# A one-core decoder layer: expert weights loaded during attention, and the two down projections of a step on separate halves of the array

## The reference, cut to what matters

```python
logits = x @ gate_w.T                      # 64 experts
topv, topi = jax.lax.top_k(logits, 8)
rw = softmax(topv)                         # weights of the 8 chosen
gu = einsum('nh,eih->nei', x, gu_w)        # gate and up, 64 + 64 columns per expert
inter = silu(gate) * up                    # 64 values per token and expert
out = einsum('nei,ehi->nh', inter_w, dp_w) # down projection, 64 -> 256
out = out + sigmoid(x @ sh_gate1_w.T) * (shared expert, same shapes)
```

## Time and profile before

| | us |
|---|---|
| median of 3 runs | 1806.1 (1800.71 to 1807.99) |
| the profiled execution, whole | 1804.36 |
| its span, first to last instruction | 1802.4 |
| PE busy | 1475.3 (82%) |
| VectorE busy | 1319.6 (73%) |
| GpSimd busy | 1109.3 (62%) |
| ScalarE busy | 694.7 (39%) |

### The profile page before, as it was taken

The page is one execution under the profiler, slowest core; times in us unless marked ns, Lnnn a source line. Parts: engine busy times, 40 slices in busy tenths (PEclk is TensorE's granted clock), DMA queues, the critical chain, the costliest instruction groups (busy, mean ns, idle before and its releaser), DMA issues. The chain is left out here.

```text
span 1802.4 us, 34145 instructions
## 1 busy us (share of the span) xinstructions
PE 1475.3 (82%) x9600; PEld 1233.7 (68%) x9600; DVE 1319.6 (73%) x3879; ACT 694.7 (39%) x1462; POOL 1109.3 (62%) x1090
## 2 busy tenths in 40 slices
PE   3679999999999899999999855779999999992000
PEld 2568888888888787888888744567777777771000
DVE  3458888888888888888888843147777765553898
ACT  3235444545453444444443412124444444441221
POOL 3328676767676667677776641027777777774444
PEclk8789999999999999999999977579999999996555
DMA  5861212121212112121212117976655556642886
GB/s 197 287 201 50 84 49 77 54 79 51 76 56 74 56 63 69 53 79 47 85 47 71 45 70 230 256 214 191 188 187 185 184 182 189 190 120 99 294 298 241
DMA packets 161421, 237.36 MB, mean 132 GB/s; under 512 B 28044, under 2 KB 135578, under 8 KB 156836
## 3 DMA queue, kind: packets, MB, share of 16 engines
q1 hardware_dynamic: 127636, 160.73, 29.2%
q0 software_dynamic: 27648, 69.28, 10.4%
q10 hardware_dynamic: 6032, 6.13, 1.0%
HBM read 127.47 MB, written 116.93 MB: 136 GB/s over the span
## 5 line engine op out<-in xcount | busy, mean ns | idle before, releaser
L1347 POOL DMA_INDIRECT expert_out_scratch<-y,target x320 | 319.1, 997 | 225.5 <-issue 107.4
L484 POOL DMA_INDIRECT slot_scratch<-xrow x256 | 272.2, 1063 | 187.8 <-DVE xrow L1100 111.6
L1438 ACT ACTIVATE x_turned<-bank_x 128x512 f32<-128x512 f32 x176 | 105.1, 597 | 281.1 <-PE bank_x L1377 281.0
L523 PE MATMUL bank_c<-wq_w,x1t 128*128 128x512 f32 x768 | 193.2, 403 | 15.4 <-DVE q_work L942 11.7
L1417 PE MATMUL bank_y<-dp,inter_t 64*128 (+1 forms) x704 | 205.7, 414 | 0.0
L1396 PE MATMUL bank_g<-gu,x_turned 128*128 (+1 forms) x1408 | 195.6, 284 | 0.0
L669 PE MATMUL bank_d<-wo_w,o2t 128*128 128x256 f32 x1536 | 193.4, 286 | 2.0 <-DVE o2t L858 2.0
L669 PEld LDWEIGHTS bank_d<-wo_w,o2t 128*128 128x128 f32 x1536 | 187.6, 192 | 3.1 <-DVE o2t L858 2.7
L1616 DVE COPY y<-bank_y 128x512 f32<-128x512 f32 x160 | 110.6, 691 | 97.1 <-PE bank_y L1417 97.1
L429 POOL TENSOR_TENSOR q_rs<-q_ve,minus_half 128x8 f32<-128x8 f32 x64 | 137.4, 2147 | 71.3 <-DVE q_ve L933 67.6
L523 PEld LDWEIGHTS bank_c<-wq_w,x1t 128*128 128x128 f32 x768 | 142.3, 190 | 56.6 <-DVE q_work L942 21.0
(11 more groups left out here) (232 smaller groups left out, 3074.0 us busy)
## 6 DMA issues: line engine op xcount, KB each, us to landing
x_rows<-slot_scratch SPq DMA_DIRECT2D x320, 136.0 KB
rows<-expert_out_scratch SPq DMA_DIRECT2D x32, 1152.0 KB, 5.6
slot_scratch<-zeros SPq DMA_DIRECT2D x18, 1088.0 KB, 11.8
gu<-in_gate_up SPq DMA_DIRECT2D x11, 768.0 KB, 12.5
expert_out_scratch<-y,target POOLq DMA_INDIRECT x320
token_row_scratch<-xrow SPq DMA_DIRECT2D x32, 136.0 KB, 1.8
x_rows<-token_row_scratch SPq DMA_DIRECT2D x16, 272.0 KB
dp<-in_down SPq DMA_DIRECT2D x22, 192.0 KB, 13.7
```

Source lines behind the costliest of these rows:

```text
L484: nc.gpsimd.indirect_dma_start(out=slot_d[:, :], out_offset=bass.IndirectOffsetOnAxis(ap=xrow[slot][:, SLOT8 + k:SLOT8 + k + 1].bitcast(U3 ...
L523: last = nc.tensor.matmul(target, left[a][:, c, :], right(b, c), start=(n == 0 and c == 0), stop=(n == len(PASSES) - 1 and c == C - 1))
L1347: nc.gpsimd.indirect_dma_start(out=y_d[:, :], out_offset=bass.IndirectOffsetOnAxis(ap=target[s % 8][:, j:j + 1], axis=0), in_=y[s % 4][:, ...
L1438: nc.scalar.activation(xt[s % 2][:, :, :, :].rearrange("p j c n -> p (j c n)"), bank_x[:, s % 2, :], ACT.Copy).then_inc(sig["x_copied"], 1)
```

## The change

Six edits go together.

1. **Place of the weights.** `gu` and `dp` are given fixed places in SBUF that overlap attention's big buffers (the query, key and value weights, `wo_w`, `o2t`, `q_work`); attention's buffers are declared in another order for it.
2. **Time of the loads.** SP loads all of `gu` at the iteration of attention in which tile 31 is projected, after the last projections, and all of `dp` at the iteration in which tile 31 is stored, after the last output projection; in both cases ahead of that iteration's `store_row` and `store_meta`. No weights are loaded by the expert phase's opening; its first steps wait on `gu_in` and `dp_in`.
3. **Two halves.** `dp` now has 128 partitions. Partitions 0 to 63 hold all 66 down matrices; partitions 64 to 127 hold a ring of 8, one per step modulo 8, and the shared expert's. The second row tile of each sparse step takes its down matrix from the ring. SP loads it with the step's rows: a third DMA per sparse step (64 rows of 1 KB, from a row index that is a second column of the table). The gated values of both row tiles are turned by one transpose of 128 x 128 instead of two of 128 x 64, so the two lie on the two halves of the partitions.
4. **`bank_y`.** Each row tile's result has a bank of its own, so there is one buffer, and `project(s)` waits for the copy of step s-1.
5. **Waits.** A row buffer's reload waits for `y_ready` of its step as well (the ring). POOL no longer waits for the row scatters at the end of attention; SP waits for them before the first sparse load.
6. **Order in the expert phase.** The tables are computed in DVE's iterations 0 to 2 instead of 0 to 6, with a third find per column for the ring's rows and four small operations more. The loads of `metas` and `slots` are issued after step 1 instead of before step 0.

```diff
+            def load_gate_up():
+                sp.wait_ge(sig["qk_projected"], TILES)
...
+                sp.wait_ge(sig["v2_projected"], TILES)
+                groups = gu[:, 0:EPAIRS * 512].rearrange("p (g n) -> p g n", g=GROUPS)
+                for g in range(GROUPS):
+                    sp.dma_start(groups[:, g, :], gate_up[g, :, :]).then_inc(weights["gu_in"], 16)
+
+            def load_down():
+                sp.wait_ge(sig["q_transposed"], 2 * TILES)
+                sp.wait_ge(sig["cross_proj"], TILES)
+                own = dp[0:INNER, :].rearrange("p (g a h n) -> p g a h n", g=GROUPS, a=GROUP, h=2)
+                for g in range(GROUPS):
+                    for h in range(2):
+                        sp.dma_start(own[:, g, :, h, :],
+                                     down[g, h * INNER:(h + 1) * INNER, :].rearrange("p (a n) -> p a n", a=GROUP))\
+                          .then_inc(weights["dp_in"], 16)
+                sp.dma_start(dp[INNER:P, 8 * D:9 * D], down[GROUPS - 1, 0:INNER, 2 * D:3 * D])\
+                  .then_inc(weights["dp_in"], 16)
...
                 at(b, store_x1)
+                if c is not None and isinstance(c.n, int) and c.n == TILES - 1:
+                    load_gate_up()
+                if e is not None and isinstance(e.n, int) and e.n == TILES - 1:
+                    load_down()
                 at_slot(e, store_row)
                 at(e, store_meta)
...
             pipeline(pool, step, ahead=ahead)
-            for slot in range(2):
-                pool.wait_ge(sig[f"scattered{slot}"], 16 * TOP_K * (TILES // 2))
...
-        dp = sb("dp", [INNER, 2, EPAIRS, D])
+        sb("dp_home", [P, DP_W])
...
-        inter_t = [sb(f"inter_t{n}", [INNER, 2 * P]) for n in range(2)]
+        inter_t = [sb(f"inter_t{n}", [P, P]) for n in range(2)]
...
                 if s >= 8:
                     sp.wait_ge(sig["x_turned"], s - 7)
+                    if sparse(s):
+                        sp.wait_ge(sig["y_ready"], s - 7)
...
             def load_sparse(s):
...
+                at = sp.snap(regs[3], min_val=0, max_val=(GROUPS * P - INNER) * GROUP + GROUP - 1)
+                sp.dma_start(dp[INNER:P, s % 8 * D:(s % 8 + 1) * D], down_rows[bass.ds(at, INNER, GROUP), :])\
+                  .then_inc(done, 16)
...
-                for j in range(2):
-                    mm = nc.tensor.transpose(bank_i[0:INNER, s % 2, j * P:(j + 1) * P], inter[s % 2][:, j, :],
-                                             identity[:, :])
-                mm.then_inc(sig["inner_turned"], 1)
+                nc.tensor.transpose(bank_i[:, s % 2, 0:P], inter[s % 2][:, :, :].rearrange("p j x -> p (j x)"),
+                                    identity[:, :]).then_inc(sig["inner_turned"], 1)
...
             def project(s):
...
                 pe.wait_ge(sig["inner_copied"], s + 1)
-                if s >= 2:
-                    pe.wait_ge(sig["y_copied"], s - 1)
-                for j in range(2):
-                    first = held[s][j][1] if sparse(s) else shared_at[1]
-                    mm = nc.tensor.matmul(bank_y[:, s % 2, j * D:(j + 1) * D], inter_t[s % 2][:, j * P:(j + 1) * P],
-                                          dp_flat[:, bass.ds(first, D)], start=True, stop=True)
-                mm.then_inc(sig["y_ready"], 1)
+                if s >= 1:
+                    pe.wait_ge(sig["y_copied"], s)
+                own = held[s][1] if sparse(s) else shared_at[1]
+                ring = s % 8 if sparse(s) else 8
+                nc.tensor.matmul(bank_y[:, 0, 0:D], inter_t[s % 2][0:INNER, :], dp[0:INNER, bass.ds(own, D)],
+                                 start=True, stop=True)
+                nc.tensor.matmul(bank_y[:, 1, 0:D], inter_t[s % 2][INNER:P, :], dp[INNER:P, ring * D:(ring + 1) * D],
+                                 start=True, stop=True).then_inc(sig["y_ready"], 1)
...
-            tables = {0: [table_counts, table_whole, table_tiles], 3: [table_opened, lambda: table_find(0)],
-                      4: [lambda: table_find(1), lambda: table_find(2)], 5: [table_depth, table_rows], 6: [table_starts]}
-            for n in range(2):
-                tables[1 + n] = [lambda k=k: table_scan(k) for k in range(3 * n, 3 * n + 3)]
+            tables = {0: [table_counts, table_whole, table_tiles] + [lambda k=k: table_scan(k) for k in range(6)],
+                      1: [table_opened] + [lambda c=c: table_find(c) for c in range(3)],
+                      2: [table_depth, table_rows, table_starts]}
```

More of the change, by code:

```diff
@@ L27 @@
 GROUPS = EPAIRS // GROUP
-GROUP = 3
-GROUPS = EPAIRS // GROUP
 XW = 272
@@ L210, in attention_phase @@
         h2_rs = sb("h2_rs", [P, 1])
-        xrow = [sb(f"xrow{n}", [P, XW]) for n in range(2)]
         zeros = sb("zeros", [P, XW])
@@ L1230, in expert_phase, with number @@
         bank_x, bank_g, bank_i, bank_y = bank("bank_x", 2), bank("bank_g", 2), bank("bank_i", 2), bank("bank_y", 2)
+        later = SHARED_STEPS - SHARED_FIRST
+        order = [("shared", k) for k in range(SHARED_FIRST)]
+        for n in range(SPARSE_STEPS):
+            order.append(("sparse", n))
+            if later and n % 16 == 15 and n // 16 < later:
+                order.append(("shared", SHARED_FIRST + n // 16))
+        steps_of = {step: s for s, step in enumerate(order)}
         def sparse(s):
-            return s >= SHARED_STEPS
+            return order[s][0] == "sparse"
+        def number(s):
+            return order[s][1]
         def y_free(s):
+            uses = sum(order[k][0] == order[s][0] for k in range(s % 4, s + 1, 4))
             if sparse(s):
-                return sig[f"y_scattered{s % 4}"], 32 * ((s - SHARED_STEPS) // 4 + 1)
-            return sig[f"y_stored{s % 4}"], 16 * (s // 4 + 1)
+                return sig[f"y_scattered{s % 4}"], 32 * uses
+            return sig[f"y_stored{s % 4}"], 16 * uses
         def rows_loaded(s):
-            return sig[f"x_in{s % 8}"], 32 * (s // 8) if sparse(s) else 16 * (s // 8 + 1)
+            return sig[f"x_in{s % 8}"], sum(48 if sparse(k) else 16 for k in range(s % 8, s + 1, 8))
         block = stack.enter_context(nc.Block())
@@ L1306, in _ @@
[L1306 to L1314 removed]
+                    at = sp.snap(regs[2 * j], min_val=1, max_val=SLOT_ROWS - P)
@@ L1315, in _ @@
                     pass_tables()
                     sp.wait_ge(sig["tables_in"], 48)
-                if s >= SHARED_STEPS - 8:
-                    load_sparse(s + 8)
-            for s in range(SHARED_STEPS + 8, STEPS):
+                    for slot in range(2):
+                        sp.wait_ge(scattered[slot], 16 * TOP_K * (TILES // 2))
                 load_sparse(s)
+            for s in range(8):
+                load(s)
+            for s in range(STEPS):
+                if not sparse(s):
+                    store_shared(s)
+                if s + 8 < STEPS:
+                    load(s + 8)
+                if s == 1:
+                    sp.dma_start(metas[:, :, :], meta_d.rearrange("(t p) e -> p t e", p=P))\
+                      .then_inc(sig["metas_in"], 16)
+                    sp.dma_start(slots[:, :, :], row_d[:, SLOT8:SLOT8 + TOP_K].bitcast(U32)
+                                 .rearrange("(t p) k -> p t k", p=P)).then_inc(sig["slots_in"], 16)
@@ L1321, in _ @@
             for n in range(4):
-                sp.wait_ge(sig[f"y_stored{n}"], 16 * (SHARED_STEPS // 4))
+                sp.wait_ge(sig[f"y_stored{n}"], 16 * sum(not sparse(s) for s in range(n, STEPS, 4)))
         @block.gpsimd
@@ L1392, in gate_and_up @@
                 for j in range(2):
-                    first = held[s][j][0] if sparse(s) else shared_at[0]
+                    first = held[s][2 * j] if sparse(s) else shared_at[0]
                     for c in range(C):
@@ L1652, in _ @@
                     stage()
-                if s == SHARED_STEPS:
+                now = s < STEPS and sparse(s)
+                if now and number(s) == 0:
                     table_slots()
-                if sparse(s) and s < STEPS:
+                if now:
                     match_row(s)
@@ L1662, in _ @@
                     copy_y(s - 3)
-                if sparse(s) and s < STEPS:
+                if now:
                     bound_row(s)
-                n = s - SHARED_STEPS - 8
+                n = number(s) - 8 if now else None
                 if n == -1:
```

210 lines of the change are left out of this document (113 added, 97 removed).

## The result

| | before | after |
|---|---|---|
| median, us | 1807.05 (4 runs) | 1751.49 (4 runs, 1746.26 to 1757.51) |
| ratio to before | | 0.9687, 95% interval 0.9654 to 0.9719 |
| profiled execution, us | 1804.36 | 1752.66 |
| opening of the expert phase | 1094.5 | 1102.3 |
| opening to first scatter | 105.9 | 67.9 |

The account below looks back on a forecast made before the run. PE was taken to bound the sparse stage, with POOL close behind, and full DMA engines the shared stage. 1804.4 less 37 (shared) and 21 (sparse) gives 1746, 1748 us on the median's scale; range 1730 to 1772.

Parts of the forecast that it names:

- PE's step: Sparse step on PE: 2.75 us less 0.44 for down products and 0.11 for one transpose, giving 2.20.
- The step from the cross-attention rows to two products per step: Down products: halves run side by side as in cross-attention's four products, so four records take 0.62 us, 0.44 less.
- Rival 4: Down products: the halves don't overlap, PE needs 2.64 us a step, result 1754; chance 0.05.
- Sparse stage: POOL sets the pace: 160 x 2.56 plus 96 x 0.10 us makes 419, 21 less than 440.
- the collisions: Sparse stage: DVE lookups falling on POOL's scatter openings cost 0.10 us in each of 96 steps, bounds 0 and 0.19.
- Rival 1: Sparse stage: POOL keeps 2.75 us a step or worse in the 96 lookup steps, result 1757 to 1782; chance 0.12.
- The ring on SP: Third DMA per sparse step: SP needs 2.3 us a step, at most 2.73; row loads land in under 10, hidden.
- Rival 2: Sparse stage: SP becomes the bound through the third DMA, 2.73 us a step, result 1766; chance 0.08.
- Shared stage: Weights leave it, tables decide: first scatter at 1163 instead of 1200.5, 37 us saved; bounds 1154 and 1180.
- Rival 3: Shared stage hardly shrinks: table chain and SP's order set it, first scatter 1185, result 1770 us; chance 0.06.
- The end of attention: Early loads hidden there; tail costs 0, bounds 0 and a 2.6 us gain from POOL's dropped wait.
- Rival 5: Sparse stage: TensorE's clock falls as PE idles; half the steps slow adds 144 us, result 1892; chance 0.04.

Follow-up runs that it names:

- run 3: Changed kernel with one scatter per sparse step, the second row block's y never scattered: 1699.0 us (total not comparable), sparse stage 371.7 us.
- run 9: Changed kernel with the loads of metas and slots issued by POOL instead of SP: 1748.0 us, ratio 0.9636 to the kernel before.
- run 1: Changed kernel with the early weight loads kept and the halves undone: 1780.2 us, ratio 0.9833 to the kernel before.
- run 4: Changed kernel with early loads kept, halves undone and one scatter per sparse step: 1768.4 us (total not comparable), sparse stage 436.0 us.
- run 10: Changed kernel with metas and slots loaded by POOL and eight of sixteen shared steps placed among the sparse ones: 1729.9 us, ratio 0.9539.
- run 11: Changed kernel with the first two stages of the weight lookup done for the first tile only: sparse stage 413.2 us.
- run 12: Changed kernel without the ring's load, the third DMA of a sparse step: sparse stage 415.5 us, shared stage 66.5 us.
- run 5: Changed kernel with six groups of down weights (12 transfers) loaded in the expert phase instead of attention: shared stage 71.3 us, on a slow chip.
- run 2: Changed kernel with halves and ring kept, expert weights loaded in the expert phase as before: 1785.0 us, ratio 0.9835 to the kernel before.
- run 6: Changed kernel with the loads of metas and slots issued by POOL, on a slow chip: 1993.8 us, shared stage 60.9 us.
- run 7: Changed kernel with half of the down weights in the expert phase and metas and slots from POOL, slow chip: 2005.6 us, ratio 0.9827.
- run 8: Changed kernel with down weights split, metas and slots from POOL, and eight shared steps among the sparse ones, slow chip: 2003.5 us, ratio 0.9818.

## Why the prediction was right

Forecast 1748, measured 1751.5. The mechanisms of both stages came out as worked out, 38.0 and 22.2 us where 37 and 21 were forecast. Some of that nearness is luck, since errors inside each stage cancel. The opening, costed at nothing, came 7.7 us later: 2.1 by the change, and 5.6 by a stretch of half clock that comes and goes without a change of code.

**PE's step.** Forecast 2.20 with 0.62 for the products, measured 2.22 and 0.63. The step from the cross-attention rows to two products per step held. Rival 4 falls. Its price was mis-reckoned: 2.64 is 0.08 above POOL's 2.56 in the 64 steps without a lookup and below the 2.66 of the others, so 5 us, not 160 x 0.04. The DMA share worked out with the ring is 0.67, not 0.68 (measured 0.70). Neither changes the forecast.

**Sparse stage.** Forecast 419, measured 417.8. Two terms were off and nearly cancel: without lookups 413.2 us remain, 2.58 a step where 2.56 was taken, 3.6 us more over the stage; the collisions cost 4.6 us, 0.05 in each of the 96 steps, where 0.10 was taken. The stretch of the earlier trace rows that gave the upper bound was denser in collisions than the rest: it holds 24 of the 26 records of before that lasted over 1.1 us. Rival 1 falls.

**The ring on SP.** Forecast 2.3 a step, upper bound 2.73; run 3 has 2.32 with SP hardly waiting. Landing: 9.0 us in the median after the issue, where under 10 was taken. Rival 2 falls, but by little: POOL's 2.6 covers SP's 2.32 by less than 0.3.

**Shared stage.** Forecast 68.5, measured 67.9, by a sum whose terms were less good than the total. The `slots` load was taken as 3 us; run 9 against after gives 7.2 for it and `metas`. The tables went out 41.5 us behind the opening, 36.5 in the forecast. From there to PE's first sparse rows it took 13.4 (1143.75 to 1157.10), 16 in the forecast, and then 13.0 to the first scatter, as forecast. The forecast's 37 us hold the gain of the loads and, by the 2.3 us a step in its working, that of the halves, without parting them. Runs 1 and 4 do: 31 to 33 are the loads', 5 to 7 the halves'. Rival 3 falls.

**The end of attention.** `gu` was hidden as said: its 11 issues took 5.7 us at 1023, and with the short stretch of half clock DVE's last residual sum came at 1067.6 to 1070.6 in the five runs with the early loads, where it came at 1068.9 before. For the tail behind that sum the forecast was 0, with a gain of up to 2.6 as its bound. From the sum to the opening it was 25.7 us before (1068.88 to 1094.54), and in after:

```profile
1074.48 0.42 DVE L1026 TENSOR_TENSOR h<-x_res,bank_d 128x256 f32<-128x256 f32 x1 [7.06 <-PE bank_d L700]
```

```profile
1102.26 0.20 POOL L1376 MEMSET identity<- 128x128 f32 x1 [8.34 <-POOLq L80]
```

27.8; runs 1, 3, 4 and 9 to 12, with the early loads too, have 27.8 to 28.2. The run without them has 24.0 (1075.93 to 1099.94). So the down weights at this place cost 3.8 us, and the rest of the change gained 1.7, which I put down to the removal of POOL's wait for its scatters (not tried alone). The forecast had that gain as a bound and held the cost for hidden ("stores of tile 31 behind it land by 1087"). SP's and DVE's timelines and SP's last wait show what holds up the last row store:

```profile
1074.54 14.88 SPq L353 DMA_DIRECT2D dp<-in_down  x22
...
1082.89 0.23 DVE L1131 MAX8 xrow<-meta 128x8 uint32<-128x64 f32 x1
...
1090.34 0.37 SPq L329 DMA_DIRECT2D token_row_scratch<-xrow  x1
...
SPq L409 <- DMA token_row_scratch<-xrow: 8.1, 1, 8.1
```

DVE has sorted the slots by 1083.1, but SP issues the 23 loads until 1090.1 and sends the store 7.2 us after that. The forecast had 15.5 us for the transfer of `dp` and none for its issue; the issue alone took 15.5, so the time of the store, counted from the sum, came out as forecast, for another reason. Its landing did not: SP waits 8.1 us for it, where the forecast had 2.6 (1084.4 to 1087). In run 5, with 11 loads ahead of it, the store went out as soon as the slots were sorted, the wait was 1.9 and the opening 2.3 us earlier; it eased both at once, so the two are not parted. That step failed, by 2.1 us net.

**Rival 5.** The clock kept 0.98 over the sparse stage, with PE idle for 44 us in it. It falls.

## What to carry to other kernels

Before making an engine faster, work out the pace of every other engine in that stage, the issuing queues too: here PE could win 0.53 us a step and the stage 0.14, and the forecast had both (0.55 and 0.13) from the trace of before. Once another engine is the bound, look for work that can be moved into the idle time of the first one: eight of the sixteen shared steps moved into the sparse stage cost nothing and gained more than the queue edit beside them (17.7 and 7.2 us). Try a load of many small pieces on a queue that has nothing else to do. And a transfer put into a "dead" stretch stands ahead of that stretch's last stores, in the issuing engine's list as well as in the queues.

## What the runs showed of the hardware

**The clock at the end of attention has two courses for one code.** The granted clock fell from full to half at 1026 to 1030 us in before, in after and in runs 1 to 4 and 9 to 12, at times for 6.8 us and at times for 20.5, and rose again. Windows of 1036 to 1046, of the halves-only run and of run 10:

```profile
1036.00:1046.00 10.00, 10.00 (x49) 9.26 (x46) 4.85 (x12) 1.36 (x3) 4.63 (x5) 0.50 0.16 54
```

```profile
1036.00:1046.00 10.00, 7.86 (x67) 7.65 (x66) 8.31 (x19) 1.06 (x1) 5.81 (x6) 1.00 1.01 399
```

The long form came in after and in runs 1, 2 and 9, the short one in before and in runs 3, 4, 10, 11 and 12. The attention code of all these runs but 2 is that of after. Run 2 has no load of weights there and has the long form; run 10 loads at 399 GB/s and has the short one. So the early loads are neither needed for it nor enough, and I count 5.6 of the 7.7 us by which after's opening is later (DVE's sum of tile 31 at 1074.5 in place of 1068.9) as chance. Each kernel was profiled once, so no kernel is seen with both forms. But run 10's profiled execution, with the short form, took 1721.3 us, and its five others 1728.6 to 1732.7. PE was busy for all of the 8 us from 1014 to 1022, at full clock, and for 4.9 to 5.5 of the next 8, in which or right behind which the clock fell, in before, after and runs 2, 3 and 10 alike; what sets the length is open.

**The same load is dear on one queue and cheap on another.** `metas` and `slots` are 4096 pieces each, of 512 and 32 bytes. On SP their issues took 0.8 and 7.9 us and that of the store behind them 4.0 in place of 0.4; on POOL 1.8 and 1.7 (run 9). The Trainium skill, DMA: Bandwidth & Descriptors, section "Why a DMA increments its semaphore by 16 and not by 1", says that one descriptor moves one contiguous run of the last dimension, which gives the two times 4096; the trace has no count of them, and why SP stands at the second load and not at the first was not tried.

**One chip was slower by 13%, and only in some stages.** On the chip of runs 5 to 8 the shared stage of run 6 took 60.9 us, as on the others (60.7), and the end behind the last scatter 162; attention was 90 us longer, and the sparse stage took 575. In it DVE's copies of y stood idle 59 times with a releaser that the profile calls remote, since it found none on the core:

```profile
L1674 DVE COPY y<-bank_y 128x512 f32<-128x512 f32 x159 | 109.3, 688 | 158.6 <-remote 127.0 <-PE bank_y L1466 23.4 <-issue 7.5
```

In after the copies' 59 waits end with the landing of a scatter (63.6 us in all), and POOL's records are hardly longer here (1002 ns in the mean, 992 in after), so it may be the landing that is slow; that is not shown. Both slow stages are those in which POOL scatters. The cause wasn't tried.
